# Delta-rule attention on one core: recurrence chunks reordered across four engines

## The reference, cut to what matters

```python
q, k, v = (silu(dwconv_causal(x @ W)) for W in (Wq, Wk, Wv))     # 16 heads of 128
a = sigmoid(x @ Wa + ba);  beta = sigmoid(x @ Wb + bb)
ks = k * D ** -0.5
def step(S, t):                        # S: batch x 16 heads x 128 x 128
    y = einsum('bhvk,bhk->bhv', S, k_t)
    err = y - v_t
    S = a_t[..., None] * S - (b_t * err)[..., None] * k_t[:, :, None, :]
    return S, einsum('bhvk,bhk->bhv', S, q_t)
o = layernorm(o) * ln_g + ln_b
o = (o * sigmoid(x @ Wg)) @ Wo
```

## Time and profile before

| | us |
|---|---|
| median of 3 runs (2782.4 to 2798.67) | 2786.93 |
| the profiled execution | 2790.64 |
| its span | 2788.7 |
| share of the span: PE, PE's weight loads, DVE, ACT, POOL | 76%, 58%, 54%, 42%, 38% |
| granted TensorE clock over the span | 0.827 |

### The profile page before, as it was taken

The page is one execution under the profiler, slowest core; times in us unless marked ns, Lnnn a source line. Parts: engine busy times, 40 slices in busy tenths (PEclk is TensorE's granted clock), DMA queues, the critical chain, the costliest instruction groups (busy, mean ns, idle before and its releaser), DMA issues. The chain is left out here.

```text
span 2788.7 us, 45057 instructions
## 1 busy us (share of the span) xinstructions
PE 2106.8 (76%) x16812; PEld 1630.0 (58%) x16824; DVE 1504.5 (54%) x3258; ACT 1177.4 (42%) x2885; POOL 1062.2 (38%) x982
## 2 busy tenths in 40 slices
PE   8596549888879958576795667965779657668798
PEld 5364226566557847465675556854558546546586
DVE  2223632266663338646676566856568566446533
ACT  3112311145453328343564435644346444325433
POOL 0223022210006525837238471385713757110154
PEclk9698779989989979666896577976779758789899
DMA  8422022200015023211222112222122221120240
GB/s 276 122 25 50 0 90 23 37 20 22 1 41 185 0 50 98 71 47 61 84 73 78 46 62 69 84 63 65 61 69 84 63 65 54 38 55 2 86 140 15
DMA packets 138316, 179.45 MB, mean 64 GB/s; under 512 B 62048, under 2 KB 114544, under 8 KB 132992
## 3 DMA queue, kind: packets, MB, share of 16 engines
q1 hardware_dynamic: 129952, 166.46, 19.4%
q0 software_dynamic: 8160, 10.26, 2.3%
HBM read 154.52 MB, written 22.17 MB: 63 GB/s over the span
## 5 line engine op out<-in xcount | busy, mean ns | idle before, releaser
L2618 DVE SCALAR_TENSOR_TENSOR XT<-M_delta,CW_delta,XT 128x256 f32<-128x256 f32 x576 | 249.7, 494 | 79.3 <-ACT M_delta L2437 49.2
L2135 PE MATMUL PS<-XP_delta,X 128*128 128x268 f32 (+1 forms) x1024 | 242.1, 389 | 15.5 <-DMA X<-in_L_attn_b_heads 15.5
L2135 PEld LDWEIGHTS PS<-XP_delta,X 128*128 128x128 f32 x1024 | 192.7, 189 | 66.7 <-DMA X<-in_L_attn_b_heads 19.6
L1541 PE MATMUL PS<-XP_rffn,UW_rffn 128*128 128x512 f32 x816 | 194.8, 395 | 5.0 <-POOL UW_rffn L1495 4.6
L1541 PEld LDWEIGHTS PS<-XP_rffn,UW_rffn 128*128 128x128 f32 x816 | 155.7, 191 | 38.8 <-issue 6.3
L1273 ACT ACTIVATE PR_attn<-PS,NM_attn 128x256 f32<-128x256 f32 (+1 forms) x384 | 130.7, 448 | 103.7 <-DVE NM_attn L1343 103.7
L2254 PE MATMUL PS<-GN_delta,TR_delta 32*128 32x64 f32 x1536 | 94.3, 419 | 82.8 <-ACT TR_delta L2553 82.8
L1495 POOL TENSOR_TENSOR UW_rffn<-W_rffn,UW_rffn 128x512 fp32r<-128x512 f32 x34 | 44.2, 1301 | 295.1 <-ACT UW_rffn L1602 295.1
L561 POOL DMA_INDIRECT sums<-XS_moe,token_moe x46 | 71.7, 1559 | 220.9 <-ACT XS_moe L661 202.0
L2589 ACT ACTIVATE S_delta<-S_delta,AO_delta 128x128 f32<-128x128 f32 x512 | 153.0, 392 | 0.0
L2166 PE MATMUL PS<-KQ_delta,TR_delta 128*128 128x64 f32 x1024 | 138.8, 283 | 12.3 <-DVE TR_delta L2635 12.1
(11 more groups left out here) (457 smaller groups left out, 5356.7 us busy)
## 6 DMA issues: line engine op xcount, KB each, us to landing
M_delta<-gram_delta SPq DMA_DIRECT2D x32, 1280.0 KB, 5.9
X<-in_L_attn_b_heads SPq DMA_DIRECT2D x64, 512.0 KB, 3.5
EW<-in_L_ffn_w SPq DMA_DIRECT2D x24, 512.0 KB, 10.2
CB_rffn<-routes_rffn SPq DMA_DIRECT2D x20, 512.0 KB, 21.9
XN<-in_L_attn_b_outs SPq DMA_DIRECT2D x16, 512.0 KB, 3.6
F_delta<-in_L_attn_b_outs SPq DMA_DIRECT2D x4, 2048.0 KB, 8.1
W_rffn<-in_L_ffn_tiles SPq DMA_DIRECT2D x4, 1536.0 KB, 11.0
slots<-pad SPq DMA_DIRECT2D x2, 2967.0 KB, 14.7
```

Source lines behind the costliest of these rows:

```text
L1541: last = nc.tensor.matmul(PS[:, 4 + 2 * n + q, :], UW[qw][:, r, (q * KD + k) * P:(q * KD + k + 1) * P], XP[qx][:, k, n * NB:(n + 1) * NB], ...
L2135: last = nc.tensor.matmul(PS[:, 1 + i, 0:B * (WIN - halo)], WH[:, r, i, k, :], XP[:, k, :, n * BT + halo:n * BT + WIN], start=(k == 0), st ...
L2618: nc.vector.scalar_tensor_tensor(TMP[:, r, i], RAW[:, r, i, :, tau:tau + BT], CW[:, i, h, tau:tau + 1], TMP[:, r, i], ALU.mult, ALU.add).t ...
```

## The change

- PE makes only the first of the six cross products ahead of the first chunk's first half and the other five behind it. ACT copies the first alone, and POOL masks the others behind the preparation of the second chunk. The mask has a tile of its own (MB) instead of a part of DF.
- POOL no longer multiplies decays into F for the first chunk nor subtracts V there; DVE does both in `base` and `chunk`. POOL's multiplication of the queries' half of M moves from `prepare(n, ci)` to `queries(n, ci)`, ahead of `prepare(n, ci + 1)`.
- DVE makes both carries at once, so that `res_d` comes ahead of the second solve.
- ACT's copies of the hops all stand ahead of the state's scaling. `cuts` becomes 0, 12, 24, 46, 64.
- `key_rows` moves from the first chunk to the second, behind its last hop. The 16 gates, before 4 in each chunk and in front of the first half of chunks 1 to 3, are now spread by GATED: heads 0 to 2 in chunk 0, 3 and 4 in chunk 1, 5 to 7 in chunk 2 and 8 to 15 in chunk 3. They stand behind the chunk's last hop, but heads 8 and 9, which stand ahead of the wait for `w_d`. ACT scales three lanes between two sigmoids.
- SP's queue is not touched.

```diff
@@ block.gpsimd: own_lanes, prepare, queries @@
-                pool.wait_ge(cn_d, z["cn_d"] + o + 1)
-                for s in range(NI - 1):
-                    x, w = BLOCKS.index((s, s + 1)), NI - 1 - s
...
+                cross_lanes(n, o, 0, 0, 1)
...
                 if jj == 0:
                     decays(n, o)
+                    return
+                if jj == 1:
                     pool.wait_ge(f_d, z["f_d"] + NS * (o + 1))
...
+            def queries(n, ci):
+
+                z, r = base_of(n), ci % 2
+                pool.wait_ge(mk_d, z["mk_d"] + ci + 1)
+                q = M[:, r, :, 1]
                 pool.wait_ge(m_in[r], 16 * (NC // 2 * n + ci // 2 + 1))
                 nc.gpsimd.tensor_tensor(q, q, by_h(DD[:]), ALU.mult).then_inc(mq_d, 1)
...
+                    queries(n, ci)
                     if ci + 1 < NC:
                         prepare(n, ci + 1)
+                    if jj == 0:
+                        for s, (first, last) in enumerate(((1, 3), (3, 5), (5, 6))):
+                            cross_lanes(n, o, s, first, last)
@@ block.tensor @@
+    GATED = (3, 5, 8, H)
+    beside = lambda o, jj: (range(NR) if jj == 1 else (), range(GATED[jj - 1] if jj else 0, GATED[jj]) if o else ())
...
                     key_products(n, o)
+                    cross_products(n, o, range(1))
                     for jj in range(NI):
                         ci = o * NI + jj
-                        gates = range(4 * jj, 4 * jj + 4) if o else ()
-                        if jj:
-                            for h in gates:
-                                gate(n, h)
-                            if o:
-                                pe.wait_ge(gate_d, z["gate_d"] + 4 * jj + 4)
+                        rows, gates = beside(o, jj)
                         first_half(n, ci)
                         if jj == 0:
-                            pe.wait_ge(cn_d, z["cn_d"] + o + 1)
-                            pe.wait_ge(f_d, z["f_d"] + NS * (o + 1))
-                            for r in range(NR):
-                                key_rows(n, o, r)
-                            pe.wait_ge(kr_d, z["kr_d"] + NR * (o + 1))
-                            for h in gates:
-                                gate(n, h)
-                            if o:
-                                pe.wait_ge(gate_d, z["gate_d"] + 4)
+                            pe.wait_ge(res_d, z["res_d"] + ci + 1)
+                            pe.wait_ge(cn_d, z["cn_d"] + 2 * o + 1)
+                            cross_products(n, o, range(1, HOPS))
+                            pe.wait_ge(cn_d, z["cn_d"] + 2 * o + 2)
                         elif jj < NI - 1:
...
+                        else:
+                            for h in gates[:2]:
+                                gate(n, h)
+                            gates = gates[2:]
                         pe.wait_ge(w_d, z["w_d"] + ci + 1)
                         if jj + 1 < NI:
                             hop(n, o, jj, jj)
-                        else:
-                            pe.wait_ge(wdec_d, z["wdec_d"] + rests(o, jj))
-                            for r in range(NR):
-                                turn(n, o, r)
+                            pe.wait_ge(nw_d, z["nw_d"] + HOPS * o + hop_no(jj, jj) + 1)
+                        for r in rows:
+                            key_rows(n, o, r)
+                        if rows:
+                            pe.wait_ge(kr_d, z["kr_d"] + NR * (o + 1))
+                        for h in gates:
+                            gate(n, h)
+                        if o:
+                            pe.wait_ge(gate_d, z["gate_d"] + GATED[jj])
+                    pe.wait_ge(wdec_d, z["wdec_d"] + rests(o, NI - 1))
+                    for r in range(NR):
+                        turn(n, o, r)
@@ block.scalar @@
-            cuts = [0, 10, 28, 46, BH]
+            cuts = [0, 12, 24, 46, BH]
...
-                        elif jj < NI - 1:
-                            for x in range(jj):
+                        if jj < NI - 1:
+                            for x in range(jj + 1):
                                 hop(n, o, jj, x)
-                        for lane in range(cuts[jj], cuts[jj + 1]):
-                            last = nc.scalar.activation(S[:, lane, :], S[:, lane, :], ACT.Copy, scale=AO[:, lane:lane + 1])
-                        if jj < NI - 1:
-                            hop(n, o, jj, jj)
-                        else:
-                            last.then_inc(sdec_d, 1)
-                            for r in range(NR):
-                                turn(n, o, r)
+                        for r in rows:
+                            key_rows(n, o, r)
+                        at = cuts[jj]
+                        for h in gates:
+                            gate(n, h)
+                            then = min(at + 3, cuts[jj + 1] - 1)
+                            if then > at:
+                                decay_state(at, then)
+                            at = then
+                        last = decay_state(at, cuts[jj + 1])
@@ block.vector: base, chunk @@
                 if jj == 0:
-                    return nc.vector.tensor_copy(out, F[:, :, q, cols])
+                    return nc.vector.tensor_tensor(out, F[:, :, q, cols], DC[:, r, :, q:q + C], ALU.mult)
...
+                if not jj:
+                    c.then(nc.vector.tensor_tensor(FK, FK, V[:, :, ci * C:(ci + 1) * C], ALU.subtract))
...
                 c.then(carry(r, 0))
+                carry(r, 1).then_inc(res_d, 1)
...
-                carry(r, 1).then_inc(res_d, 1)
```

More of the change, by code:

```diff
@@ L1728, in delta_attention @@
     ZB = sb("ZB", [P, 4 * QU], BF16)
+    MB = sb("MB", [P, NI, 4, B])
     AO = sb("AO", [P, BH])
@@ L2207, in key_products, with cross_products @@
                 last.then_inc(ch_mm, 1)
-                for x, (old, new) in enumerate(BLOCKS):
+            def cross_products(n, o, blocks):
+                for x in blocks:
+                    old, new = BLOCKS[x]
                     cols = slice(new * C, (new + 1) * C)
-                    bank, first = (1 + x, 0) if x < 4 else (6, (x - 4) * 4 * QU)
+                    bank, first = (x, 0) if 0 < x < 5 else (6, x // 5 * 4 * QU)
                     for i in range(4):
@@ L2246, in hop @@
                 last.then_inc(nw_mm, 1)
-                pe.wait_ge(gn_d, z["gn_d"] + rests(o, s) + 1)
-                if s == 0 and not jj:
-                    pe.wait_ge(res_d, z["res_d"] + NI * o + 1)
+                pe.wait_ge(gn_d, z["gn_d"] + NI * o + (s + 2 if jj else 1))
                 pe.wait_ge(nw_d, x)
@@ L2544, in answer, with gate, decay_state @@
                 nc.scalar.copy(V[:, :, ci * C:(ci + 1) * C], PS[:, 5, :].rearrange("p (n t) -> p n t", t=C)).then_inc(o_d, 1)
-            def gates(n, jj):
-                for h in range(4 * jj, 4 * jj + 4):
-                    act.wait_ge(gate_mm, base_of(n)["gate_mm"] + h + 1)
-                    nc.scalar.activation(GATES[:, h // 2, h % 2], PS[:, 6 + h % 2, 0:B * BT], ACT.Sigmoid).then_inc(gate_d, 1)
+            def gate(n, h):
+                act.wait_ge(gate_mm, base_of(n)["gate_mm"] + h + 1)
+                nc.scalar.activation(GATES[:, h // 2, h % 2], PS[:, 6 + h % 2, 0:B * BT], ACT.Sigmoid).then_inc(gate_d, 1)
+            def decay_state(first, last):
+                for lane in range(first, last):
+                    done = nc.scalar.activation(S[:, lane, :], S[:, lane, :], ACT.Copy, scale=AO[:, lane:lane + 1])
+                return done
             def hop(n, o, jj, s):
@@ L2565, in _ @@
                         ci = o * NI + jj
+                        rows, gates = beside(o, jj)
                         if jj:
                             answer(n, ci - 1)
-                            if o:
-                                gates(n, jj)
                         if jj == NI - 1:
@@ L2579, in _ @@
                         if jj == 0:
-                            for r in range(NR):
-                                key_rows(n, o, r)
-                            if o:
-                                gates(n, jj)
+                            cross_products(n, o)
                             act.wait_ge(ds_d, z["ds_d"] + o + 1)
-                        elif jj < NI - 1:
-                            for x in range(jj):
+                        if jj < NI - 1:
+                            for x in range(jj + 1):
                                 hop(n, o, jj, x)
-                        for lane in range(cuts[jj], cuts[jj + 1]):
-                            last = nc.scalar.activation(S[:, lane, :], S[:, lane, :], ACT.Copy, scale=AO[:, lane:lane + 1])
-                        if jj < NI - 1:
-                            hop(n, o, jj, jj)
-                        else:
-                            last.then_inc(sdec_d, 1)
-                            for r in range(NR):
-                                turn(n, o, r)
+                        for r in rows:
```

(4 more changed lines are left out.)

37 lines of the change are left out of this document (22 added, 15 removed).

## The result

The changed kernel takes 2845.61 us (median of 4 runs, 2836.73 to 2848.51), the kernel before beside it 2792.80 us (4 runs): a ratio of 1.018, 95% interval 1.012 to 1.024. It is slower, as forecast, and the time lies in the range, though it only just reaches the forecast case's own 2845 to 2895; the loss is 53 us against 80 forecast. The profiled execution took 2836.73 us with a span of 2834.8.

A forecast was written before the change was run, and what follows sets the result against it. No engine was full; DVE's waits for hops, `first_half` products and POOL's F, 50 us a block, were the target. 4 x 24 - 4 x 4 = +80 on the profiled 2790.6 gives 2870.6, median 2867 us; range 2810 to 2900.

The forecast's parts named there:

- the forecast case: Whole kernel slower, at 2867 us, with its own range of 2845 to 2895; chance 60%.
- Second halves: The four second halves: about +24 us each, with bounds of +5 and +30.
- to the third: Second half, second w to third: M waits behind the moved fourth gate in SP's queue; +10.1 us.
- to the fourth: Second half, third w to fourth: M of the fourth chunk waits for eight gates; +7.4 us.
- Item 1: Second half up to the second w: cross products replace key rows and four gates ahead of the first hop; -5.3 us.
- The clock's gain: Second half, PE: three of ten gates, at the ends of bursts, run at 2.4 GHz; -2.3 us.
- First halves: The four first halves: hops, NH4 and F gain 11.4 us, partly offset; about -4 each, between -10 and +2.
- ACT's heap: First halves: key rows, scalings and copies on ACT delay NH4, 5.1 us in the third chunk, 2.6 in the fourth.
- Item 4: End of a second half: gates and a wait for weights stand ahead of the turn, 14.4 us less 0.3 absorbed; +14.
- M in time after all: Rival: M's place in the queue is hidden, or half the stretches run fast; 2827 us, chance 18%.
- PE at 2.4 GHz: Rival: PE runs the chunks at the upper clock, hop chain 4.0 to 2.6 us; 2767 us, chance 9%.
- The worse rival: ACT's heap and the landing both at upper bounds, first halves +2, second halves +28; 2910 us, chance 9%.

The follow-up runs named there:

- e1: The changed kernel, but SP issues M of a second half's third and fourth chunk ahead of its wait for four (eight) gates; 2809.83 us.
- e2: The changed kernel with the gates of a second half grouped 4, 4, 4, 4 instead of 3, 2, 3, 8, SP's queue as it was; 2773.88 us.
- e6: As e5, with ACT's 64 scalings split 14, 6, 22, 22 instead of 12, 12, 22, 18; 2751.65 us.
- e12: As e9, with every group of second-half gates one chunk later, the last four between fourth half solve and turn, scalings 10, 20, 22, 12; 2721.64 us.
- e9: As e5, with the key rows back in the first chunk behind its last hop and the scalings split 10, 18, 18, 18; 2742.34 us.
- e4: The kernel before with only ACT's copy of a chunk's last hop moved ahead of the state's scalings; 2752.37 us.
- e3: The changed kernel with both edits: gates by four as e2 and M issued ahead of the wait for gates as e1; 2773.88 us.
- e5: As e2, with second-half gates of chunks 2 to 4 back ahead of the half solves on PE and behind ACT's answer copy; 2765.26 us.
- e8: As e2, with second-half gates between the older chunks' hops and the wait for w, and scalings split 14, 6, 22, 22; 2774.18 us.
- e7: As e4, plus the first chunk's columns of F done by DVE and POOL's queries product moved, nothing else of the change; 2763.33 us.
- e11: As e10, with the gates of heads 4 to 7 behind the second chunk's last hop and scalings split 1, 12, 28, 23; 2770.83 us.
- e10: As e9, with the scalings split 1, 20, 22, 21 instead of 10, 18, 18, 18; 2756.60 us.

## Why the prediction was right

- *Second halves, +24 forecast, +21.1 measured.* Item by item, mean of four: up to the second w -6.5 (forecast -5.3), to the third +9.2 (+10.1), to the fourth +6.2 (+7.4), the end +12.2 (+14). In the block that the earlier trace rows came from it is -7.5, +9.6, +7.2, +13.6. Item 1 has a slip: its terms for the cross products make 6.8 and its sum takes off 7.8; with 6.8 it gives -6.3, about the mean measured. The clock's gain came at the end: the last four gates took 5.2 to 5.4 where I had 6.5, and the two ahead of the weights 2.00 in three blocks, against 3.78 in this one and 3.3 forecast. The mechanism, M behind a wait for a gate in SP's queue, is shown by e1 and e2.
- *First halves, -4 forecast, -5.8 measured.* By the waits of the half shown, the gains came in full: the hops' 10.4 became 3.8, the first chunk's wait for NH4 4.0 became 0.65, and the second chunk's 2.4 for POOL's F went. Two costs were mis-sized. ACT's heap: in the third chunk the answer is late by 3.7 and NH4 by 0.7 beyond it, in the fourth by 0.8 and 2.2. With the 1.1 for F, which I had expected to vanish from first halves, and less the 1.0 for NH4 that each of these chunks had before, that is 4.6 and 2.0 against 5.1 and 2.6. And the product that replaced DVE's copy of F cost 1.2 to 2.2 more than the copy in a first half, against 0.5 (last section); that error leaned the other way. e6 shows that the heap is real. I had named `first_half`'s products as what is waited for; it is the answer copy, one place earlier in the same queue.
- *What the sum left out.* The stretches outside the halves are 16 us shorter in all. Item 4 let the wait for the update absorb 0.3. The addition came 5.1 behind the turn and now 3.8 (1727.42 to 1731.17), since DVE has long ended the answers' chain when the turn comes: 1.3 of the 1.2 to 2.5 us that a block gains there. The rest is open: the stretch from w to the second half takes 36.5 to 44.5 us in the kernels here, without a pattern that an edit explains, and the 5.2 us behind the last turn I did not trace. From the last turn to the end it takes 380.5 us here, 380.9 in e1 and 381.4 in e12, where gates hold the turn up too, and 383.2 to 396.6 in all others, so a late turn seems to get a part back; no run isolates it.
- *Sum:* -7 from the first halves, -12 from the second ones, -16 from outside, of +80: +45, and +46 in the span. What was off is the sizing, by terms of 1 to 3 us most of which leaned to the same side, and the stretches outside the halves, which the sum put at nearly nothing. The step from 46 in the span to 53 between the medians is scatter between executions: the profiled one is the fastest of the four.
- *The rivals.* "M in time after all" fell with DVE's eight waits for M, 15.0 to 17.6 us each; e1, in which M is in time, took 2810, where that rival had 2827. "PE at 2.4 GHz" fell: the third chunk's granted clock is 0.55, and gates took 1.68 us each (26.9 / 16). Against it I had a first half "at 0.50 throughout"; that holds for its second and third chunk, while its first has 0.68. The worse rival's 2910 is 2907 by its own sum. The Trainium skill, page "TensorE: Matmul & The Clock Gate", section "HAM oscillation — how this bites in real kernels", which the prediction drew on, has waits for DMA between bursts put the array back to the lower clock. The row of 0.50 that I set beside it has no wait for DMA in it, and e1 speaks against M's waits as a cause here: with them gone the four second halves ran at 0.61 to 0.65, and at 0.60 to 0.65 in the changed kernel. e9's ran at 0.68 to 0.73, with other groups of gates and the key rows elsewhere; what keeps PE low in the changed kernel was not isolated. The same half in e1 and in e9:

```profile
1602.20:1706.88 104.68, 63.42 (x654) 49.13 (x654) 63.27 (x152) 40.88 (x129) 53.19 (x44) 0.61 0.19 64
1585.80:1673.10 87.30, 56.48 (x654) 45.13 (x653) 59.11 (x140) 40.89 (x129) 52.86 (x44) 0.73 0.22 73
```

- *The change's own idea* was right in parts that the total hid. Hop copies ahead of scalings: -40 alone (e4). Cross products behind the first half, with POOL's work and the carry moved, made first halves 3 us shorter each (e2 against e4), while second halves grew by 5.5, with the answer late behind key rows, gates and scalings. With the groups by four the whole change is a gain over the kernel before (e2); only the groups 3, 5, 8, 16 made a loss of it, 72 us.

## What to carry to other kernels

A transfer that nobody waits for can become the bound by an edit that never touches its queue: list what each queued issue stands behind, and which compute step frees that. Take a bundle of moves apart before judging it; here one move was worth 40 us and one tuple cost 72. When a wait is removed, expect a part of it (17 of 33.5 us in e1) to return from the queue that it had hidden, and place work on an in-order engine by what waits behind it, not by that engine's idle time.

## What the runs showed of the hardware

- A product of two SBUF tiles on DVE, 128x512 (the first chunk's `base`, L2678), took 0.69 to 0.70 us in the eight executions of it that no Gram product on POOL overlapped, and 1.92 to 2.93 us in the eight that one did. Each of these eight ended 0.55 to 0.56 us behind POOL's product, however early it had started, and the same holds in e1 to e3, e5, e6 and e8 to e12; in e7, where the two don't meet, all 16 took 0.69 to 0.70. In the kernel before, the copy with one SBUF tile that stood there took 0.68 to 0.70 beside POOL's product. DVE, then POOL, after the change:

```profile
1502.03 2.93 DVE L2678 TENSOR_TENSOR PS<-F_delta,DC_delta 128x512 f32<-128x512 f32 x1
1501.51 2.89 POOL L2102 TENSOR_TENSOR M_delta<-M_delta,DD_delta 128x1280 f32<-128x1280 f32 x1
```

- A kernel's own scatter differs from kernel to kernel: the runs of e7, e11 and e12 (7, 9 and 6 of them) spread over 29, 25 and 32 us, those of e4 and e10 (4 each) over 5. A part of it lies ahead of all that was edited: the delta sublayer's first instruction starts at 986.0 to 992.7 us in the 14 profiled executions. I would not tell two such kernels apart by less than 10 us from a handful of runs.
